# LoRA factors by float32 products from raw loads, another order of loads, and a router's terms on GpSimd

## The reference

```python
# first block, per sequence (expert_ids: one of 8)
hidden = relu(x @ wi.T + 2 * (x @ common_wi_a.T) @ common_wi_b.T + 2 * (x @ Wa[e].T) @ Wb[e].T)
y = hidden @ wo.T + 2 * (hidden @ common_wo_a.T) @ common_wo_b.T + 2 * (hidden @ Va[e].T) @ Vb[e].T
# second block
probs = softmax(mean_over_tokens(y) @ gate_w)
top_w, top_i = top_k(probs, 2);  top_w = top_w / top_w.sum()
out = x + sum(top_w[k] * (gelu(y @ w1[i] + b1[i]) @ w2[i] + b2[i]) for k, i in enumerate(top_i))
```

## Time and profile before

| what | value |
| --- | --- |
| median of 3 runs | 273.38 us (273.11 to 273.49) |
| the profiled execution | 273.11 us, of it 271.0 us span |
| TensorE busy | 265.3 us, 98% of the span |
| VectorE, ScalarE, GpSimd busy | 164.5, 171.4, 143.5 us |
| DMA | 19.00 MB, mean 70 GB/s |
| mean granted TensorE clock | 0.998 |

### The profile page before, as it was taken

The page is one execution under the profiler, slowest core; times in us unless marked ns, Lnnn a source line. Parts: engine busy times, 40 slices in busy tenths (PEclk is TensorE's granted clock), DMA queues, the critical chain, the costliest instruction groups (busy, mean ns, idle before and its releaser), DMA issues.

```text
span 271.0 us, 3615 instructions
## 1 busy us (share of the span) xinstructions
PE 265.3 (98%) x1168; PEld 214.5 (79%) x1168; DVE 164.5 (61%) x276; ACT 171.4 (63%) x276; POOL 143.5 (53%) x171
## 2 busy tenths in 40 slices
PE   8999999999999999998999999999999999999995
PEld 2687888888888888886888788888788888888883
DVE  1764436243389635659495686566965667665664
ACT  2655453364635459986986977776766776775650
POOL 0084342553846677799509999466366366431100
PEclk9999999999999999999999999999999999999999
DMA  5998320201013022102110222112022015000004
GB/s 160 276 309 183 101 77 0 81 1 39 4 52 124 19 80 78 57 21 79 44 36 6 74 80 77 35 42 81 12 67 77 20 60 191 2 1 2 0 0 156
DMA packets 17170, 19.00 MB, mean 70 GB/s; under 512 B 1984, under 2 KB 14528, under 8 KB 17152
## 3 DMA queue, kind: packets, MB, share of 16 engines
q1 hardware_dynamic: 16304, 17.60, 21.8%
q10 hardware_dynamic: 848, 1.18, 1.4%
HBM read 16.67 MB, written 2.10 MB: 69 GB/s over the span
## 4 chain that ended last, share of the span: by engine, by line
PE 97%; DVE 1%; issue 1%; ACT 1%; DVEq 0%; ACTq 0%
PE out_ps L661 16%; PE out_ps L665 16%; PE out_ps L662 16%; PE hid_ps L661 15%; PE hid_ps L662 15%; PE hid_ps L665 15%; PE hid_ps L814 3%; PE hid_ps L768 1%; PE hid_ps L781 1%; DVE term_lo L963 1%; ACT hid_hi L539 0%; ACT hid_ps L525 0%; DVE x_sb L1107 0%; PE out_ps L768 0%; DVEq L121 0%
## 5 line engine op out<-in xcount | busy, mean ns | idle before, releaser
L388 POOL TENSOR_TENSOR up_lo<-up_raw,up_hi 128x512 fp32r<-128x512 f32 x39 | 50.4, 1311 | 49.1 <-ACT up_hi L493 49.0
L661 PE MATMUL out_ps<-hid_hi,down_hi 128*128 128x512 f32 x192 | 74.9, 390 | 0.0
L662 PE MATMUL out_ps<-hid_lo,down_hi 128*128 128x512 f32 x192 | 74.7, 389 | 0.0
L665 PE MATMUL out_ps<-hid_hi,down_lo 128*128 128x512 f32 x192 | 74.7, 389 | 0.0
L661 PE MATMUL hid_ps<-act_hi,up_hi 128*128 128x512 f32 x176 | 68.9, 392 | 0.0
L662 PE MATMUL hid_ps<-act_lo,up_hi 128*128 128x512 f32 x176 | 68.7, 390 | 0.0
L665 PE MATMUL hid_ps<-act_hi,up_lo 128*128 128x512 f32 x176 | 68.5, 389 | 0.0
L525 ACT ACTIVATE hid_ps<-hid_ps,bias_sb 128x512 f32<-128x512 f32 x64 | 42.2, 659 | 30.7 <-DVE hid_ps L933 20.4
L909 DVE SCALAR_TENSOR_TENSOR hid_lo<-hid_ps,mix,hid_hi 128x512 fp32r<-128x512 f32 x64 | 47.8, 748 | 18.6 <-ACT hid_hi L539 18.0
L394 POOL TENSOR_TENSOR down_lo<-down_raw,down_hi 128x512 fp32r<-128x512 f32 x24 | 31.6, 1318 | 44.2 <-ACT down_hi L503 44.1
L539 ACT ACTIVATE hid_hi<-hid_ps,mix 128x512 fp32r<-128x512 f32 x64 | 44.1, 689 | 4.9 <-ACT hid_ps L525 0.4
(11 more groups left out here) (81 smaller groups left out, 208.1 us busy)
## 6 DMA issues: line engine op xcount, KB each, us to landing
up_raw<-in_w SPq DMA_DIRECT2D x16, 256.0 KB, 3.1
down_raw<-in_w SPq DMA_DIRECT2D x16, 256.0 KB, 2.6
down_raw<-in_woT SPq DMA_DIRECT2D x8, 256.0 KB, 4.6
lora_raw<-in_lora SPq DMA_DIRECT2D x10, 192.0 KB, 7.6
up_raw<-in_wiT SPq DMA_DIRECT2D x7, 256.0 KB, 7.3
outT<-x_sb SPq DMA_DIRECT2D x6, 256.0 KB, 3.2
x_sb<-in_xT SPq DMA_DIRECT2D x1, 1024.0 KB, 11.5
x_sb<-in_xT ACTq DMA_DIRECT2D x2, 256.0 KB, 4.8
```

The costliest lines, as they stand in the source:

```text
L388: ins = eng.tensor_tensor(up_lo[:, n, cols], up_raw[:, n, cols], f32(up_hi[:, n, cols]), ALU.subtract)
L661: eng.matmul(out, w_h, a_h, start=start, stop=False, skip_group_check=onto)
L662: eng.matmul(out, w_h, a_l, start=False, stop=False, skip_group_check=onto)
L665: return eng.matmul(out, w_l, a_h, start=False, stop=stop, skip_group_check=onto)
```

## The change

The first two up products of the LoRA factors (sets 0 and 1) are made in plain float32 from the first 32 rows, unsplit, out of two new small loads (`lora_first`, 64 KB, and `lora_second`, 32 KB; `raw_up_factor`). Lots 0 and 2 are still loaded and split, since later sets need them, but later. Warm-up is 12 products instead of 22 + 6. The second half of x's first token tile is loaded by SP behind the two small loads, not by ScalarE; then follow up weights 1, x's second token tile, lora (0,1), down weights 0, lora (0,0), lora (0,3), up weights 2, lora (0,2). Set 0's tiles up run in pairs (`first_pair`), with the products that need the low weights last, and `down_factor(0)` behind all of them. x's second tile is copied in two halves; two of the four low parts of x go to GpSimd. On ScalarE lora (0,1) is copied after the first two `hid_high`, lora (0,0) after it, lora (0,3) after `hid_high(0, 3)` and lora (0,2) after `hid_high(1, 0)`; on GpSimd the low parts of lora (0,2) stand behind those of lora (0,3). For both routers the token total, the product with the gate (now one float32 tile `term`) and the low terms are made by GpSimd; ScalarE only rounds `term`, in one operation.

```diff
--- before.py
+++ after.py
@@ -109,14 +109,13 @@
     SUM_LO_AT = {7: [(1, 0), (1, 1), (1, 2), (1, 3)], 13: [(2, 0), (2, 1)], 14: [(2, 2), (2, 3)]}
-    LORA_HI_AT = {0: [(0, 3)], 1: [(0, 4)], 2: [(1, 0), (1, 1)], 3: [(1, 2), (1, 3)], 4: [(1, 4)]}
-    LORA_LO_AT = {0: [(0, 3)], 1: [(0, 4)], 2: [(1, 0)], 3: [(1, 1), (1, 2)], 4: [(1, 3), (1, 4)]}
+    LORA_HI_AT = {1: [(0, 4)], 2: [(1, 0), (1, 1)], 3: [(1, 2), (1, 3)], 4: [(1, 4)]}
+    LORA_LO_AT = {0: [(0, 3), (0, 2)], 1: [(0, 4)], 2: [(1, 0)], 3: [(1, 1), (1, 2)], 4: [(1, 3), (1, 4)]}
...
     LOT = 2 * SW
-    WARM_UP = 22
-    WARM_MORE = 6
+    WARM_UP = 12
...
         def sb(name, shape, dt=F32):
@@ -228,7 +233,7 @@
-        LORA_HI = [(0, 0), (0, 2), (0, 1)] + [lot for q in sorted(LORA_HI_AT) for lot in LORA_HI_AT[q]]
+        LORA_HI = [(0, 1), (0, 0), (0, 3), (0, 2)] + [lot for q in sorted(LORA_HI_AT) for lot in LORA_HI_AT[q]]
         def lots_of(side, q):
@@ -303,15 +313,20 @@
             e = number(ids[0:1, 0:1])
-            load_lora(0, 0, e)
+            eng.dma_start(lora_first[:, :], lora[bass.ds(e, 1), 0:G, 0:LOT].rearrange("e r c -> (e r) c"))\
+               .then_inc(s_lora_first, 16)
+            eng.dma_start(lora_second[:, :], lora[bass.ds(e, 1), 0:G, 2 * LOT:2 * LOT + SW].rearrange("e r c -> (e r) c"))\
+               .then_inc(s_lora_second, 16)
+            load_x0(eng, 1)
+            next_up(1)
...
                .then_inc(s_x0b, 16)
-            load_lora(0, 2, e)
-            next_up(1)
...
             next_down(0)
+            load_lora(0, 0, e)
...
             next_up(2)
+            load_lora(0, 2, e)
@@ -417,6 +432,25 @@
+            def logit_terms(b):
+                eng.wait_ge(s_y, NT * KD * (b + 1))
+                if b == 0:
+                    eng.wait_ge(s_gate, 16)
+                eng.tensor_tensor(tok_all[:, b, :], tok_sum[:, b, 0, :], tok_sum[:, b, 1, :], ALU.add).then_inc(s_tok, 1)
+                eng.wait_ge(s_tok, b + 1)
+                if b:
+                    eng.wait_ge(s_term_hi, b)
+                eng.tensor_tensor(term[:, :, :], gate_sb[:, :, :], tok_all[:, b, :].unsqueeze(2).to_broadcast([P, KD, E]),
+                                  ALU.mult).then_inc(s_term, 1)
+            def term_low(b):
+                eng.wait_ge(s_term_hi, b + 1)
+                if b:
+                    eng.wait_ge(s_logit, b)
+                eng.tensor_tensor(term_lo[:, :, :], term[:, :, :], f32(term_hi[:, :, :]), ALU.subtract)\
+                   .then_inc(s_term_lo, 1)
             def after(sem_count):
@@ -425,14 +459,19 @@
-            after((s_rank, 1))
+            x0_low(eng, 1, 0)
+            up_low(1)
+            x0_low(eng, 1, 1)
+            after((s_x0lo[1], NT))
             lora_low(0, 1)
-            up_low(1)
...
                 if q < N_COND - 1:
+                    if q in TOTAL_AT:
+                        logit_terms(TOTAL_AT[q])
+                        term_low(TOTAL_AT[q])
@@ -450,7 +489,11 @@
                         weight_sums(q + 2)
+                    if q in LOGITS_AT:
+                        term_low(LOGITS_AT[q])
                     down_low(q)
+                    if q in TOTAL_AT:
+                        logit_terms(TOTAL_AT[q])
@@ -465,10 +508,9 @@
-            def x0b_high():
+            def x0b_high(kd):
                 eng.wait_ge(s_x0b, 16)
-                second = act_hi[:, 0, 0:4, :].rearrange("p (k t) c -> p k t c", t=NT)[:, :, 1, :]
-                eng.activation(second, x_sb[:, :, half(0, 1)], ACT.Copy).then_inc(s_x0hi, 1)
+                eng.activation(act_hi[:, 0, kd * NT + 1, :], x_sb[:, kd, half(0, 1)], ACT.Copy).then_inc(s_x0hi, 1)
             def lora_high(b, lot):
@@ -569,14 +611,10 @@
             def term_high(b):
-                eng.wait_ge(s_gate, 16)
-                eng.wait_ge(s_tok, b + 1)
+                eng.wait_ge(s_term, b + 1)
...
                     eng.wait_ge(s_logit, b)
-                for kd in range(KD):
-                    eng.activation(term_hi[:, kd, :], gate_sb[:, kd, :], ACT.Copy, scale=tok_all[:, b, kd:kd + 1])\
-                       .then_inc(s_term_hi, 1)
+                eng.activation(term_hi[:, :, :], term[:, :, :], ACT.Copy).then_inc(s_term_hi, 1)
             def router_exp(b):
@@ -592,22 +630,19 @@
             load_up(eng, 0)
-            load_x0(eng, 1)
             x0_high(0)
-            lora_high(0, 0)
...
             up0_high(1)
-            lora_high(0, 2)
-            x0b_high()
+            up_high(1)
+            x0b_high(0)
+            x0b_high(1)
+            hid_high(0, 0)
+            hid_high(0, 1)
             lora_high(0, 1)
-            hid_high(0, 0)
-            up_high(1)
-            hid_high(0, 1)
+            lora_high(0, 0)
+            hid_high(0, 2)
             down_high(0)
-            hid_high(0, 2)
-            others(0)
@@ -616,8 +651,12 @@
                 hid_high(q - 1, 3)
+                if q == 1:
+                    lora_high(0, 3)
...
                     hid_high(q, 0)
+                    if q == 1:
+                        lora_high(0, 2)
@@ -691,19 +730,34 @@
             def first_low(q):
-                return up_lo_made(q) if q else None
+                return up_lo_made(q)
+            def first_pair(t):
+                for kd in range(KD):
+                    eng.wait_ge(s_x0hi, t * KD + kd + 1)
+                    eng.wait_ge(s_up0hi, kd + 1)
+                    for f in range(2):
+                        w = up_hi[:, 0, block(kd * 2 + f)]
+                        eng.matmul(hid_ps[:, 2 * t + f, :], w, act_hi[:, 0, kd * NT + t, :], start=(kd == 0), stop=False)
+                    eng.wait_ge(s_x0lo[kd], t + 1)
+                    for f in range(2):
+                        w = up_hi[:, 0, block(kd * 2 + f)]
+                        eng.matmul(hid_ps[:, 2 * t + f, :], w, act_lo[:, 0, kd * NT + t, :], start=False, stop=False)
+                for f in range(2):
+                    for kd in range(KD):
+                        eng.wait_ge(s_up0lo, kd + 1)
+                        ins = eng.matmul(hid_ps[:, 2 * t + f, :], up_lo[:, 0, block(kd * 2 + f)],
+                                         act_hi[:, 0, kd * NT + t, :], start=False, stop=(kd == KD - 1))
+                    ins.then_inc(s_up, 1)
             def plain_tile(q, j):
...
                 for kd in range(KD):
-                    if q == 0 and (j, kd) == (3, 1):
-                        down_factor(0, out_ps[:, 3, :])
-                    if q == 0:
-                        eng.wait_ge(s_x0lo, (kd if t == 0 else KD + kd) + 1)
-                        eng.wait_ge(s_up0hi, kd + 1)
                     ins = up_product(q, kd * 2 + f, kd * NT + t, j, kd == 0, kd == KD - 1,
-                                     (s_up0lo, kd + 1) if q == 0 else first_low(q) if j + kd == 0 else None)
+                                     first_low(q) if j + kd == 0 else None)
...
             def one_of_seven(q, what, bank, start):
@@ -759,6 +813,19 @@
+            def raw_up_factor(q, *outs):
+                eng.wait_ge(s_lora_first, 16)
+                if q:
+                    eng.wait_ge(s_lora_second, 16)
+                own = lora_second[:, :] if q else lora_first[:, SW:2 * SW]
+                for kd in range(KD):
+                    ins = eng.matmul(outs[kd], lora_first[:, block(kd)], own, start=True, stop=True)
+                    if q == 0:
+                        ins.then_inc(s_prod0, 1)
+                if q:
+                    ins.then_inc(s_prod, 1)
             def up_factor(q, *outs):
@@ -815,13 +879,11 @@
             warm_up(WARM_UP)
-            up_factor(0, out_ps[:, 0, 0:SW], out_ps[:, 1, 0:SW])
-            warm_up(WARM_MORE)
-            plain_tile(0, 0)
-            plain_tile(0, 1)
-            up_factor(1, out_ps[:, 2, 0:SW], out_ps[:, 2, SW:2 * SW])
-            plain_tile(0, 2)
-            plain_tile(0, 3)
+            raw_up_factor(0, out_ps[:, 0, 0:SW], out_ps[:, 1, 0:SW])
+            raw_up_factor(1, out_ps[:, 2, 0:SW], out_ps[:, 2, SW:2 * SW])
+            first_pair(0)
+            first_pair(1)
+            down_factor(0, out_ps[:, 3, :])
@@ -1022,37 +1065,30 @@
             eng.tensor_scalar(ones[:, :], y_sb[:, 0, 0:P], 0.0, 1.0, ALU.mult, ALU.add).then_inc(s_ones, 1)
-            x0_low(0, 0)
-            lora_low(0, 0)
-            x0_low(1, 0)
+            x0_low(eng, 0, 0)
...
             up0_low(1)
-            lora_low(0, 2)
-            x0_low(0, 1)
-            x0_low(1, 1)
             merge_up(1, out_ps[:, 2, :])
+            x0_low(eng, 0, 1)
...
             hid_low(0, 2)
+            lora_low(0, 0)
...
                     router_second(FIRST_AT[q])
-                if q in TOTAL_AT:
-                    token_total(TOTAL_AT[q])
...
                 hid_low(q, 0)
-                if q in LOGITS_AT:
-                    term_low(LOGITS_AT[q])
...
```

(29 more changed lines are left out.)

13 lines of the change are left out of this document (3 added, 10 removed).

## The result

The changed kernel takes 273.94 us (median of 8 runs, 273.84 to 274.86), the kernel before, on the same chip, 273.15 us (8 runs, 272.94 to 273.62). The ratio is 1.0031, 95% interval 1.0019 to 1.0042: **slower by 0.79 us**, where 273.1 and "no change" were forecast. The profiled execution took 273.91 us, of it 272.1 span; before it was 273.11 and 271.0. The span grew by 1.1 us, the time by 0.8, since 1.8 us lie outside the span instead of 2.1.

A forecast was written before the change was run, and what follows sets the result against it. The prediction took TensorE, with 97% of the chain, as the bound. A router gain of 1.37 us and a start loss of 1.14 us summed to -0.23: 272.9 us profiled, 273.1 as median, range 272.2 to 274.4.

The forecast's parts named there:

- X: Start: landing time of x's second token tile, taken as 10.9 us; the loss at set 1's down correction was counted from it.
- the line from X: Start: ScalarE copies, then GpSimd's lows of lot 1, then TensorE; down_factor(0) at X + 4.65.
- The router: Second router: low terms made on GpSimd remove TensorE's wait, 1.51 - 0.14 = 1.37 us gained.
- The float32 products: Start: four unsplit products of 256 columns at 0.5 us each, from 6.3 to 8.4.
- rival D: Start: fewer warm-up products leave float32 at the slow pace, +1.1 us on top, 274.2; chance 0.08.
- The landings: Start: first x tile's second half at 8.1 to 8.6, x's second tile at 10.9, first real product at 9.2 to 9.6.
- The line behind it: From down_factor(0): down(0,0) 3.4 later; lot 2's copy behind hid_high(1,0) makes TensorE wait over 1 us; down_factor(1) at 23.55.
- A: The forecast case: X between 10.6 and 11.7, both effects nearly cancel, 272.8 to 273.9 us; chance 0.41.
- B: x's second tile lands nearly as before, X at 10.3: -0.83 us, 272.5; chance 0.33.
- C: x's second tile lands by SP's own order, X at 12.05: +0.92 us, 274.3; chance 0.13.

The follow-up runs named there:

- router_only: Kernel before with only the change's router part (total, gate product, low terms on GpSimd, one ScalarE copy), old start: 271.47 us against 273.16, ratio 0.9938.
- x0low_dve: Changed kernel with the low-part subtraction x0_low(1, 0) on VectorE, ahead of up0_low(0), instead of GpSimd: 273.71 us, ratio 1.0019 to the kernel before.
- combo: Changed kernel with lora lot (0,2) copied before hid_high(1,0), and x0_low(1, 0) and x0_low(1, 1) on VectorE: 272.83 us, ratio 0.9978 to the kernel before.
- final_warm: `final` with 17 warm-up products in place of 14: 271.41 us, ratio 0.9927 to the kernel before.
- lot2_early: Changed kernel with ScalarE's copy of lora lot (0,2) put right behind lot (0,3), before hid_high(1,0): 272.80 us, ratio 0.9989 to the kernel before.
- x0_act: Changed kernel with the second half of x's first tile loaded from ScalarE's queue again: 273.54 us, ratio 1.0019 to the kernel before.
- final: `combo` with 14 warm-up products; x's second tile and lora (0,1) moved ahead on ScalarE, lora_low(0,1) before up_low(1) on GpSimd: 272.42 us, ratio 0.9956 to before.
- x011_dve: Changed kernel with the low-part subtraction x0_low(1, 1) on VectorE instead of GpSimd: 274.27 us, ratio 1.0026 to the kernel before.
- start_only: Changed kernel with both routers put back as before on VectorE and ScalarE: 275.48 us, ratio 1.0083 to the kernel before.

## Why the prediction was wrong

The step that failed is the line from X, the landing of x's second tile, to `down_factor(0)`. Most of the rest came out as written.

- **The router** was right: 1.51 - 0.14 = 1.37 us forecast and seen, 1.4 in `router_only`. GpSimd's operation of 16 columns took 0.22 us, for which 0.3 was taken.
- **The float32 products** were right: four of them from 5.96 to the end of the group near 7.95, 0.50 each, each with two records. TensorE's pace had risen before them this time (granted clock 1.00 from 5 to 9 us), so rival D did not come about. By the four passes that the Trainium skill gives for true FP32 ("FP8 and Floating Point Precision", TensorE Precision Notes) and the 0.12 us of a reduced-precision product of 256 columns, an estimate is 0.48; the trace agrees.
- **The landings** were right: the half tile at 7.97 (8.1 to 8.6 forecast), x's second tile at 10.83 (10.9), the first real product at 9.08 (9.2 to 9.6).
- **The line from X to `down_factor(0)` failed**: 15.55 forecast, 16.59 measured. Lot 1's low parts were to start at X + 2.95 = 13.85 and started at 15.00. (a) 0.7 of it is ScalarE: the line let its copies start at X, though the change puts `up_high(1)` ahead of them; this waits for VectorE's merge, that for the low weights, these for the half tile. Lot 1's copy (13.77, 0.6) ended at 14.4, not at 13.7. (b) The other 0.5 is GpSimd: `up_low(1)` and `x0_low(1, 1)` stand ahead of `lora_low(0, 1)` and end at 14.92 (13.18 + 1.74), 0.4 after that copy's low parts could have started. The working priced neither move: it took the time at which an operand is ready, not that at which the engine is free. Inside (a) is a price that no row of before had: VectorE's subtraction beside one of GpSimd takes 1.30 instead of 0.41 us. `x0low_dve` shows that part as 0.34 at `down_factor(0)`; `combo`, with GpSimd's queue shortened too, gave 0.88 (15.71), most of the 1.04, and the mended order another 0.8 in `final_warm`. How the 1.04 splits between (a) and (b) is read from the one trace. And the line left a branch out altogether: the change puts `down_factor(0)` behind all of set 0's products, and these wait for both low parts of the second tile (13.77 and 14.92), so TensorE was not free before 16.47 either. By this trace, lot 1 on time would have won 0.1 us alone.
- **The line behind it** was right in its mechanism and 0.2 short: `down(0,0)` 3.6 behind `down_factor(0)` (3.4 forecast), the copy of lot 2 at 22.34 right behind `hid_high(1, 0)`, a wait of 1.0. `lot2_early` took it out at its full price.
- **The rivals.** Net of the median, I had written the time as a function of X alone. With X as forecast the sum was 1.2 us short, so A, B and C all measured the wrong variable for this kernel; in `x0_act_warm` and `final_warm`, where other waits were gone, X was the start of the chain. The low clock, rival D's mechanism, was real, but not in this kernel's median: of its eight runs those at a mean clock of 1.0 took 273.84 and 273.91, those at 0.992 to 0.994 273.89 to 274.12, probably because TensorE waits there anyway, which no trace of those runs shows (one at 0.987 took 274.86). It came out in the versions whose waits were gone.

## What to carry to other kernels

A chain over engines is costed from each engine's *order*, not from when its operand is ready: for every link write down what stands ahead on the same queue and what that waits for, and take the later of the two. When a step goes to GpSimd, ask what VectorE does in those same microseconds; here two subtractions side by side cost more than one after the other on VectorE. Look for a second branch that ends as late as the one you cost: taking out one of two can show next to nothing. And when warm-up products are cut, look at the granted clock of the products that follow, over several runs: here three more products at the start took `final` from 272.42 to 271.41 us, and without them a better order showed little but a wider scatter.

## What the runs showed of the hardware

- **VectorE and GpSimd block each other.** VectorE's 128 x 256 subtraction started at 8.96, GpSimd's at 8.70; VectorE's ended at 10.26, 0.28 after GpSimd's end at 9.98. At 12.42 VectorE's 128 x 512 took 1.35 in place of 0.69 with `up_low(1)` (11.94 to 13.21) beside it, and GpSimd's next one, from 13.18, took 1.74 in place of 1.28. In each pair the one that began later ended after the other by less than it needs alone. That looks like waiting, not like sharing. The Trainium skill ("SBUF — State Buffer", section "Who interferes with whom") says that a VectorE instruction with two SBUF inputs contends with a GpSimd one that reads SBUF, and calls the port pair that they share an exclusive lock; the trace agrees. That the one that issues first holds it for the whole instruction is said there of VectorE's 2-port modes; these rows fit it too.
- **The granted clock can fall again soon after it has risen.** In the profiled runs of `x0_act` and `final` it was 0.50 to 0.59 for some 4 us, in that of `x011_dve` 0.50 for over 6, behind 12 or 14 warm-up products, the narrow float32 products and waits of 0.3 to 1.2 us around them. Other runs of the same kernels kept it up; in 18 runs with 17 warm-up products the mean was never under 0.998. Between the medians of the runs at 0.994 and those at 0.998 or more lie 1.0 us in `combo` and 1.3 in `final`. The Trainium skill ("TensorE: Matmul & The Clock Gate", section "What's actually happening") says that the default state is throttled and activity releases it; the trace agrees in direction. Whether it is the waits or the narrow products that bring it down was not tried apart.
- **Time outside the span** is 2.0 to 2.2 us in all runs of the kernel before and 1.7 to 1.9 in all runs of the changed kernel and of every version, `router_only` and `start_only` alike. It is 0.3 us of every gain here, and no run explains it.
